# A decoder layer on one core: ternary weight blocks are transposed raw, their signs are taken while the bank is emptied, and every engine gets a new order

## What is computed

```python
x = layernorm(x + attention(x))          # windows of 128 rows, 16 heads of 16
x = layernorm(x + scan_layer(ctx, x))    # selective scan, 512 channels, 16 states
x = layernorm(x + feed_forward(x))       # ternary weights

# scan_layer, per batch:
u = silu(conv(in_proj @ ctx) + conv_b);  dt, Bm, Cm = split(x_proj @ u)
delta = softplus(dt_proj @ dt + dt_b);   A = -exp(A_log)
state = state * exp(delta * A) + (delta * u) * Bm      # over 512 steps, for 16 states
y = (sum over states of state * Cm + D * u) * silu(x)

# feed_forward:
xq = quantised(rms_norm(x))
p  = silu(xq @ sign(W_g).T) * (xq @ sign(W_u).T)
out = p @ sign(W_d).T
```

## Time and profile before

| quantity | value |
|---|---|
| median of 3 runs | 962.4 us |
| profiled execution, span | 964.3 us |
| VectorE busy | 852.1 us, 88% |
| TensorE matmul busy | 836.9 us, 87% |
| ScalarE busy | 682.8 us, 71% |
| GpSimd busy | 445.2 us, 46% |

### The profile page before, as it was taken

How to read it: one execution, slowest core, us unless ns; L and a number is a source line. 1 busy time by engine, 2 the same in 40 slices (tenths; PEclk the granted TensorE clock), 3 DMA queues, 4 the chain that set the end, 5 groups by cost and what they waited for, 6 DMA issues and landing times.

```text
span 964.3 us, 12713 instructions
## 1 busy us (share of the span) xinstructions
PE 836.9 (87%) x4258; PEld 526.9 (55%) x4258; DVE 852.1 (88%) x1168; ACT 682.8 (71%) x1148; POOL 445.2 (46%) x260
## 2 busy tenths in 40 slices
PE   6979787788888898999889888999889899884997
PEld 3447566574455565655456555654456556563453
DVE  2499999998899999999999999898989999987554
ACT  4875655665897788866897888766878788772532
POOL 2065745542265755553356655454345655453000
PEclk9995867789989989999998999899979998977999
DMA  8222252320101111001001111001000010000000
GB/s 228 79 71 82 75 180 85 101 64 0 46 23 34 66 36 36 29 1 56 13 23 34 67 43 34 22 1 35 11 23 33 23 43 31 28 12 0 12 22 23
DMA packets 29216, 43.93 MB, mean 46 GB/s; under 512 B 6128, under 2 KB 10096, under 8 KB 29152
## 3 DMA queue, kind: packets, MB, share of 16 engines
q1 hardware_dynamic: 26512, 42.52, 13.9%
q10 hardware_dynamic: 2640, 0.59, 0.3%
HBM read 38.78 MB, written 4.33 MB: 45 GB/s over the span
## 4 chain that ended last, share of the span: by engine, by line
DVE 50%; PE 27%; issue 15%; ACT 6%; POOL 1%; DMA 1%; DVEq 0%; POOLq 0%; ACTq 0%
DVE h L1519 18%; DVE acc L1536 12%; DVE s_pT L1402 3%; PE bank_a L2274 3%; PE bank_f L2422 3%; DVE neg_max L1408 2%; PE bank_m L2398 2%; PE bank_f L2499 2%; DVE p_lo L1600 2%; PE bank_a L2301 2%; DVE g_p L1596 2%; DVE h L1451 2%; PE bank_m L2362 2%; DVE st L1422 2%; PE bank_a L2319 1%
## 5 line engine op out<-in xcount | busy, mean ns | idle before, releaser
L524 POOL TENSOR_TENSOR b_x<-u,b_row 128x1024 f32<-128x1024 f32 x124 | 340.3, 2753 | 263.1 <-DVE h L1519 261.9
L1519 DVE TENSOR_TENSOR_SCAN h<-d_a,b_x 128x1024 f32<-128x1024 f32 x128 | 292.5, 2302 | 0.0
L2398 PE MATMUL bank_m<-ident,h 128*128 128x128 f32 x1024 | 173.8, 304 | 47.9 <-DVE acc L1536 41.9
L1536 DVE SCALAR_TENSOR_TENSOR acc<-bank_m,c_cols,acc 128x512 f32<-128x512 f32 x256 | 186.1, 740 | 6.5 <-PE bank_m L2398 5.3
L893 ACT ACTIVATE d_a<-delta,a_neg 128x511 f32<-128x511 f32 x256 | 168.6, 712 | 28.6 <-DVE h L1519 28.1
L2398 PEld LDWEIGHTS bank_m<-ident,h 128*128 128x128 f32 x1024 | 130.8, 158 | 89.7 <-DVE acc L1536 44.7
L936 ACT ACT_TABLE_LOAD x46 | 59.0, 1283 | 46.2 <-PE bank_f L2422 45.9
L512 POOL TENSOR_TENSOR rs<-ve,neg_half 128x1 f32<-128x1 f32 (+1 forms) x36 | 30.9, 859 | 131.0 <-DVE neg_mean L1617 70.5
L814 ACT ACTIVATE s_pT<-s_pT,neg_max 128x128 f32<-128x128 f32 x256 | 81.5, 390 | 11.9 <-DVE neg_max L1408 11.4
L2301 PE MATMUL bank_a<-k_par,qT 32*128 32x256 f32 x256 | 80.1, 436 | 2.5 <-DVE s_pT L1402 1.3
L2319 PEld LDWEIGHTS bank_a<-v_aug,s_pT 128*128 128x128 f32 x512 | 73.7, 220 | 8.3 <-issue 6.3
(11 more groups left out here) (182 smaller groups left out, 1458.5 us busy)
## 6 DMA issues: line engine op xcount, KB each, us to landing
b_row<-bc_rows SPq DMA_DIRECT2D x64, 256.0 KB, 3.2
x_next<-in_x_dram SPq DMA_DIRECT2D x4, 1024.0 KB, 5.7
y<-in_L_ffn_W_g_dram SPq DMA_DIRECT2D x16, 256.0 KB, 2.7
xn<-in_L_ffn_W_u_dram SPq DMA_DIRECT2D x16, 256.0 KB, 3.0
g_p<-in_L_ffn_W_d_dram SPq DMA_DIRECT2D x16, 256.0 KB, 3.2
out_dram<-y SPq DMA_DIRECT2D x16, 256.0 KB, 2.7
cx<-in_ctx_dram SPq DMA_DIRECT2D x4, 512.0 KB, 5.2
acc<-n_L_xattn_in_proj_w_dram ACTq DMA_DIRECT2D x1, 512.0 KB, 5.3
```

The source lines that it names most:

```text
L524: nc.gpsimd.tensor_tensor(b_x[:, half], du[:, halves(half)], b_row[:, n % 2].unsqueeze(1).to_broadcast([P, EH, S]), ALU.mult)\
L1519: nc.vector.tensor_tensor_scan(flat(h[:, (n + 1) % 2, halves(half)]), flat(d_a[:, half]), flat(b_x[:, half]), 0.0, ALU.mult, ALU.add).then ...
L1536: nc.vector.scalar_tensor_tensor(acc[:, i], bank_m[bank][:], c_cols[:, i, bass.ds(n, 1)], acc[:, i], ALU.mult, ALU.add).then_inc(m_free[ba ...
L2398: last = tr(bank_m[bank][:, c * P:(c + 1) * P], h[:, (n + 1) % 2, c, i * P:(i + 1) * P], ident[:])
```

## The change

It has three parts.

First, the way of a weight block. TensorE transposes the raw f32 block straight from its load buffer. ScalarE takes the signs while it empties the bank and writes fp8 or f16 into `wgT`, `wuT` or `wdT`. The sixteen-bit sign buffers, the f16 identity, the semaphores `sgn_ready` and VectorE's 48 copies are gone. A load of the next block of the same matrix now waits until this block's transposes are done.

Second, some waits. `du_0` and `du_1` wait for all four `skip_T`, where they waited for the last one in the order. A scan waits until the transposes of the state two before are done. `quantise` and `round_rows` wait for earlier steps of their own chains.

Third, the orders. The five lists are written out anew for every batch (`first_front`, `batch_0` to `batch_3`, `last_feed_forward`). Each helper is called as often as before with the same arguments, apart from VectorE's `weights_T`. In eleven places of batches 1 to 3 the sync engine issues `spread(b, n)` behind `spread(b, n + 1)`.

```diff
             def weight_block(w, j, i):
                 n = w * 4 + j
                 if n:
-                    sp.wait_ge(sgn_ready[i], n)
+                    sp.wait_ge(f_full[i], n + 1)
...
             def du_1(b):
-                pool.wait_ge(a_full[2], (2 * TT + 1) * b + 1)
+                for full, use in ((f_full[0], f_skip(b)), (f_full[1], f_skip1(b)), (f_full[2], FC + b if b else 0),
+                                  (a_full[2], (2 * TT + 1) * b)):
+                    pool.wait_ge(full, use + 1)
...
             def sign(w, j, i):
-                act.wait_ge(w_in_sem[i], 16 * (4 * w + j) + 16)
-                if w or j:
-                    act.wait_ge(f_full[i], 1 + 4 * w + j)
-                nc.scalar.activation(w_sgn[i][:], w_raw[i][:], ACT.Sign).then_inc(sgn_ready[i], 1)
+                cols = bass.ds((w * 4 + j) * P, P)
+                dst = (wgT[:, :, cols], wuT[:, :, cols], wdT[:, j * FQ:(j + 1) * FQ, bass.ds(w * P, P)])[i]
+                act.wait_ge(f_full[i], 1 + 4 * w + j + 1)
+                nc.scalar.activation(dst, bank_f[i][:].rearrange("p (k n) -> p k n", k=4), ACT.Sign,
+                                     saturate=False if i < 2 else None).then_inc(f_free[i], 1)
...
             def scan(b, n, half):
+                if n >= 2:
+                    dve.wait_ge(m_full[1], M_BATCH * b + M_FRONT + 2 * (n - 2) + 2)
...
-            def weights_T(w, j, i):          # VectorE
-                dve.wait_ge(f_full[i], 1 + 4 * w + j + 1)
-                nc.vector.tensor_copy(dst, bank_f[i][:].bitcast(dt)[:, 0:4 * P].rearrange("p (k n) -> p k n", k=4),
-                                      saturate=False if i < 2 else None).then_inc(f_free[i], 1)
...
             def weights_T(w, j, i):          # TensorE
-                pe.wait_ge(sgn_ready[i], n + 1)
+                pe.wait_ge(w_in_sem[i], 16 * n + 16)
                 pe.wait_ge(f_free[i], n + 2)
-                    last = tr(bank_f[i][:].bitcast(dt)[:, k * P:(k + 1) * P], w_sgn[i][:, k * P:(k + 1) * P], eye[:])
+                    last = tr(bank_f[i][:, k * P:(k + 1) * P], w_raw[i][:, k * P:(k + 1) * P], ident[:])
...
+                spread(2, 13)                # sync engine, end of batch_2
+                next_rows(3)
+                store(1, 1)
+                spread(2, 15)
+                spread(2, 14)
```

More of the change, by code:

```diff
@@ L739, in _ @@
[L739 to L748 removed]
+                root3(0)
+                inputs(1, 7, 0)
+                inputs(1, 7, 1)
+                inputs(1, 8, 0)
+                inputs(1, 8, 1)
+                root1(1, 0)
+                inputs(1, 9, 0)
@@ new lines, in batch_1 @@
+                scan(1, 3, 0)
+                gather(1, 1, 3)
+                add_bias(1, 1, 1)
+                product(0, 3)
+                row_max(1, 1, 0)
+                gather(1, 2, 0)
+                context(1, 0)
+                gather(1, 2, 1)
+                scan(1, 3, 1)
+                row_max(1, 1, 1)
+                quantised_T(1)
+                low(0, 3)
+                gather(1, 2, 3)
+                gather(1, 2, 2)
+                scan(1, 4, 0)
+                gather(1, 3, 1)
@@ new lines, in batch_1 @@
+                gather(1, 3, 0)
+                product(1, 0)
+                scan(1, 4, 1)
+                add_bias(1, 1, 2)
+                gather(1, 3, 3)
+                gather(1, 3, 2)
+                scan(1, 5, 0)
+                low(1, 0)
+                residual1(1, 0)
+                gather(1, 4, 0)
+                residual3(0, 0)
+                scan(1, 5, 1)
+                product(1, 1)
+                add_bias(1, 1, 3)
+                statistics3(0)
+                low(1, 1)
@@ new lines, in batch_1 @@
+                gather(1, 4, 2)
+                gather(1, 4, 1)
+                row_max(1, 1, 2)
+                row_max(1, 1, 3)
+                gather(1, 4, 3)
+                product(1, 2)
+                gather(1, 5, 0)
+                scan(1, 6, 0)
+                scan(1, 6, 1)
+                gather(1, 5, 1)
+                gather(1, 5, 2)
+                add_bias(1, 2, 0)
+                low(1, 2)
+                scan(1, 7, 0)
+                row_max(1, 2, 0)
+                gather(1, 5, 3)
@@ new lines, in batch_1 @@
+                quantise(2, 0, 2)
+                scan(1, 7, 1)
+                product(1, 3)
+                statistics1(1, 0)
+                gather(1, 6, 1)
+                gather(1, 6, 0)
+                add_bias(1, 2, 1)
+                gather(1, 6, 3)
+                low(1, 3)
+                context(1, 1)
+                gather(1, 6, 2)
+                row_max(1, 2, 1)
+                quantised_T(2)
+                scan(1, 8, 0)
+                scan(1, 8, 1)
+                gather(1, 7, 0)
@@ new lines, in batch_1 @@
+                gather(1, 7, 1)
+                product(2, 0)
+                add_bias(1, 2, 2)
+                gather(1, 7, 3)
+                gather(1, 7, 2)
+                row_max(1, 2, 2)
+                residual3(1, 1)
+                low(2, 0)
+                scan(1, 9, 0)
+                add_bias(1, 2, 3)
+                gather(1, 8, 1)
+                row_max(1, 2, 3)
+                residual1(1, 1)
+                product(2, 1)
+                gather(1, 8, 0)
+                scan(1, 9, 1)
@@ new lines, in batch_1 @@
+                low(2, 1)
+                gather(1, 8, 3)
+                statistics3(1)
+                gather(1, 8, 2)
+                gather(1, 9, 1)
+                statistics1(1, 1)
+                gather(1, 9, 0)
+                product(2, 2)
+                gather(1, 9, 3)
+                scan(1, 10, 0)
+                scan(1, 10, 1)
+                gather(1, 9, 2)
+                add_bias(1, 3, 0)
+                quantise(3, 0, 3)
+                gather(1, 10, 0)
+                low(2, 2)
```

3801 lines of the change are left out of this document (2432 added, 1369 removed).

## The result

| | before | after |
|---|---|---|
| median | 962.6 us (4 runs, 957.9 to 969.3) | 996.9 us (4 runs, 992.1 to 1003.1) |
| profiled execution, span | 964.3 us | 995.9 us |

The ratio of after to before is 1.034, with a 95% interval from 1.027 to 1.041. The forecast was 937 us, with 0.07 on slower.

The account below looks back on a forecast made before the run. VectorE bounds the scan stretches, with TensorE close behind in batch 0. Terms of -2, -16, -5 and -2 sum to -25 us: 939.3 from the 964.3 us span, 937 as median; 8-in-10 range 920 to 957.

Parts of the forecast that it names:

- Both signs that I had named for being wrong: Batch 0 gains under 8 us, or batches 1 to 3 move by more than 14 us in either direction.
- Batches 1 to 3, -2: Batches 1 to 3 and tail: new order lists save 2 us, within bounds of -14 and +14.
- Batch 0, -16: Scan stretch of batch 0: falls from 155 to 139 us as VectorE's copies go; floor 133.5.
- VectorE busy 94% of batch 0: Batch 0, first to last scan: some 139 us with VectorE busy 94%; near 85% means TensorE or ScalarE bounds it.
- First seam, -5: First seam: 3.9 us of copies and a 2.1 us wait go, of which 5 us are counted.
- Front, -2: Before the first scan: four VectorE copies, 2.3 us, are removed; new waits cost 0.
- ScalarE's sign, 0: ScalarE's sign read from a bank: 586 to 688 ns against 623, -1.8 to +3.1 us over 48, counted as 0.
- Loads, 6 to 12 us of TensorE's waits: Batch 0: later reloads make TensorE wait 12 times 0.5 to 1 us, included in the 139 us.
- Tail, 0: Tail: TensorE bounds it and its work is unchanged, so 0 us.
- TensorE takes over in batch 0: Batch 0: clock mix stays, transposes add up to 16 us, stretch stays about 155; total 953 us, chance 0.19.
- Rows of B one state late: Batches 1 to 3: eleven later spreads delay scans, 65 us if uncovered, total 1002; 2 to 3 expected; chance 0.06.

Follow-up runs that it names:

- e1: Kernel before, its engine orders kept, with the new way of the weight blocks and the new waits: 961.0 us, ratio 0.994.
- e2: Changed kernel with the second scan put right behind the first in 25 states: 1025.9 us, ratio 1.064.
- e8: Changed kernel with the rows of B brought in rising order again in eleven places: 998.0 us against 996.9.
- e12: Changed kernel with the order of the kernel before up to the end of batch 0, whole products: 992.2 us, ratio 1.028.
- e3: Changed kernel with GpSimd's product cut to 64 of 512 columns, all orders kept: 954.6 us, ratio 0.991.
- e11: Changed kernel with the order of the kernel before up to the end of batch 0, product cut to 64 of 512 columns: 951.4 us, ratio 0.987.
- e5: Kernel before with the second scan put behind two short VectorE operations in 18 states: 998.2 us, ratio 1.036.

## Why the prediction was wrong

The sum was -2 - 16 - 5 - 2 = -25 us. Both signs that I had named for being wrong came: batch 0 gained nothing, and batches 1 to 3 moved by more than 14 us. By its steps:

- *Batches 1 to 3, -2 with bounds of 14 either way: the step that failed.* It measured +27.4. I wrote that the work is the same, and bounded what an order can do by VectorE's idle time, 28.4 us. The work was the same only because the old order kept scans out of products. The time of an instruction was taken as fixed where it depends on what another engine does at its start. Short products in the same order take 35 us off (538.0 to 502.9).
- *Batch 0, -16: the floor was wrong.* It measured +6.2. I took VectorE's own busy time and its present idle time, 133.5 us, for the floor. Scan and product exclude each other and take turns: at 4.65 us from one scan's end to the next one's, 32 of them are 149 us, and e1's batch 0 took 152.8. So at most 9 us could be had in an order in which scans and products alternate; e1 had 5. The lock is not the whole of it, since 148.2 remains with short products, where VectorE is idle 12 us of batch 0. The new order adds its own wait for TensorE: 162.2 against 147.7. The term was also too large from the start: the copies' records overlap their neighbours', and leaving them out of before's trace frees 16.3 us of VectorE in this stretch, not 21.5 (21.4 in all, not 27.7). In after these 16.3 us stand against 16.6 more of held scans and 7.3 more of idle time.
- *The sign "VectorE busy 94% of batch 0"* came true, 154.2 of 164.1 us, in a stretch that was meant to take 139: held time reads as busy.
- *First seam, -5*: it measured -2.8 with the new orders and 0 with the old ones (51.8 in both before and e1), where the copies' 4 us turned to waits. Half right.
- *Front, -2*: the first scan starts at 59.4 us where it started at 59.3. But this start spreads by 4 us over the profiled executions: 55.4 in e2 and 59.0 in e8, which have the front of after, and 57.1 in e1, 53.8 in e12. Single executions can't judge a term of 2.
- *ScalarE's sign, 0*: 592 to 595 ns against 621 to 625. Right, and inside its bounds.
- *Loads, 6 to 12 us of TensorE's waits*: TensorE's weight loads wait 1.6 + 0.6 us for them. They were dearer in the forecast than in the run.
- *Tail, 0*: 94.0 against 95.1. Right.
- *TensorE takes over in batch 0 (the first rival)*: its condition came in part only. The clock was 0.83, not 0.76, but VectorE, freed of held scans, is busy 138.2 of 162.2 us in e3, the share of 85% that I had named as its sign. It is true of the new order, and not of the old one (e11: 147.7).
- *Rows of B one state late (the slower rival)*: the waits came, 33 us where under 5 were expected, and by e8 they cost nothing. Slower happened, by another mechanism, to which I had given no chance at all. The clue was within: a product with a mean of 2753 ns, of whose spread I did not ask.
- *Small slips*: VectorE's least idle time in a scan stretch is 2.7 us (152.3 of 155), not 1.8. The spread of 0.5% came from three executions; 25 of the kernel before ran from 957.5 to 971.1 us, which is 1.4%. Neither changes the sum.

## What to carry to other kernels

Before an order is changed, list the pairs of instructions on different engines that lengthen each other, and look at the spread of the durations within a group, not at its mean: a scan of 2.28 us that sometimes takes 4.1 is a dependence that no semaphore shows. The floor of a stretch is then the sum of both partners, not the busy time of one. And when a profile's busy time grows while its instructions become fewer, the group whose mean rose is the place to start. To test such a cause, shorten the partner and leave the order alone: both runs that moved instructions (e2, e5) changed TensorE's waits by more than the thing under test.

## What was not expected of the hardware

- Held time is booked as busy time of the held engine: VectorE reads 88% in both kernels.
- The hold is by the instruction: with products of 1.27 us the held time went from 48.6 to 25.0 us.
- A stretch with the same orders and the same work takes 175.3 or 167.5 us at a granted clock of 0.88 or 0.97 (batch 3, before and e1, which only adds waits there). Why the clock differs is open.
- The records of successive VectorE instructions overlap: 48 copies whose own records cover 27.7 us add 21.4 us to the engine's busy time.
- With 133 transposes fewer in batch 0 its granted clock was 0.69 instead of 0.79, and TensorE was busy 3 us less (one execution each). Why the clock fell was not tested.
